# A two-layer decoder kernel: the norms' last step goes from VectorE to GpSimd, two more block loads go ahead of the stores, and two square roots go behind a wide product

## The reference, cut to what matters

```
x = _layernorm(x + self_attention_0(x))          # 16 heads of 8, rotary positions, causal
x = _layernorm(x + cross_attention_0(x, ctx))    # 16 heads of 8, key mask
x = _layernorm(x + experts(x))                   # 8 experts, each token takes 2, hidden width 512
x = _layernorm(x + self_attention_1(x))          # 16 heads of 64, not causal
x = _layernorm(x + cross_attention_1(x, ctx))    # 16 heads of 8, key mask
x = _layernorm(x + ternary_ffn(x))               # weights in {-1, 0, 1}, gelu, an inner norm over 512

def _layernorm(x, axis=-1, eps=1e-05):
    m = jnp.mean(x, axis=axis, keepdims=True)
    v = jnp.var(x, axis=axis, keepdims=True)
    return (x - m) / jnp.sqrt(v + eps)
```

## Time and profile before

| what | us |
|---|---|
| three runs | 410.81, 412.69, 412.75 |
| their median | 412.69 |
| the profiled execution, whole | 409.98 |
| its span, first to last instruction | 408.0 |
| PE busy in the span | 347.2 (85%) |
| DVE busy | 252.6 (62%) |
| POOL busy | 186.3 (46%) |
| ACT busy | 183.7 (45%) |
| mean granted clock of TensorE | 0.946 of full |

### The profile page before, as it was taken

How to read it: one execution, slowest core, us unless ns; L and a number is a source line. 1 busy time by engine, 2 the same in 40 slices (tenths; PEclk the granted TensorE clock), 3 DMA queues, 4 the chain that set the end, 5 groups by cost and what they waited for, 6 DMA issues and landing times.

```text
span 408.0 us, 9801 instructions
## 1 busy us (share of the span) xinstructions
PE 347.2 (85%) x3718; PEld 263.3 (65%) x3718; DVE 252.6 (62%) x592; ACT 183.7 (45%) x386; POOL 186.3 (46%) x267
## 2 busy tenths in 40 slices
PE   3889899998970899898986874899999989999892
PEld 2556666665870889898975561756667565667572
DVE  1799988896554125732353776435566567887894
ACT  2466676664672422222221251433454335667541
POOL 1767666655455245433227633102222247452673
PEclk9999999996996799999996988699999999999998
DMA  6799900000381011111111100000000000000000
GB/s 199 238 307 300 292 2 2 2 2 28 96 261 39 27 53 40 39 40 53 29 31 42 34 19 2 0 2 2 2 2 2 2 2 2 2 2 2 2 26 26
DMA packets 35938, 22.95 MB, mean 56 GB/s; under 512 B 4142, under 2 KB 33846, under 8 KB 35766
## 3 DMA queue, kind: packets, MB, share of 16 engines
q1 hardware_dynamic: 34582, 19.63, 16.7%
q0 software_dynamic: 1024, 2.10, 1.7%
q10 hardware_dynamic: 288, 0.62, 0.5%
HBM read 14.60 MB, written 7.73 MB: 55 GB/s over the span
## 4 chain that ended last, share of the span: by engine, by line
PE 58%; DVE 14%; issue 8%; POOL 7%; ACT 5%; DMA 5%; SPq 1%; POOLq 0%; DVEq 0%; ACTq 0%
PE banks L426 7%; PE banks L821 6%; PE banks L546 5%; PE banks L523 4%; PE banks L1500 4%; PE banks L1508 4%; PE banks L1531 4%; PE banks L808 4%; DMA XG<-routed_rows 3%; PE banks L852 3%; POOL KB L670 2%; PE banks L530 2%; DVE mx L400 2%; PE banks L495 2%; PE banks L507 2%
## 5 line engine op out<-in xcount | busy, mean ns | idle before, releaser
L330 POOL TENSOR_SCALAR ve<-mv 128x1 f32<-128x1 f32 x40 | 10.6, 265 | 93.8 <-DVE mv L325 93.8
L670 POOL TENSOR_TENSOR KB<-KT,cst 128x512 f32<-128x512 f32 x48 | 49.3, 1047 | 7.5 <-DVE KT L630 5.6
L435 ACT ACTIVATE PT<-banks 128x512 f32<-128x512 f32 x64 | 34.9, 595 | 33.3 <-PE banks L426 32.3
L1523 DVE TENSOR_TENSOR PT<-banks,PR 128x512 f32<-128x512 f32 x23 | 15.9, 691 | 46.6 <-PE banks L1508 40.0
L400 DVE TENSOR_REDUCE mx<-banks 128x16 f32<-128x1024 f32 x32 | 38.7, 1209 | 7.9 <-PE banks L530 5.6
L858 ACT ACTIVATE U<-banks 128x512 f32<-128x512 f32 x40 | 23.9, 597 | 42.5 <-PE banks L821 22.1
L426 PE MATMUL banks<-cst,PR 128*128 128x128 f32 x256 | 36.6, 289 | 6.5 <-POOL PR L887 6.5
L1488 POOL COPY U<-WALL 128x1024 f32 x21 | 21.8, 1040 | 43.8 <-PE banks L1508 42.2
L426 PEld LDWEIGHTS banks<-cst,PR 128*128 128x128 f32 x256 | 29.0, 146 | 10.2 <-POOL PR L887 7.6
L808 PE MATMUL banks<-XT,WQKV 128*128 128x128 f32 x256 | 34.9, 300 | 0.4 <-ACT XT L1703 0.4
L416 ACT ACTIVATE PR<-PR 128x1024 f32<-128x1024 f32 x32 | 33.8, 1057 | 3.1 <-DVE PR L410 2.8
(11 more groups left out here) (181 smaller groups left out, 699.1 us busy)
## 6 DMA issues: line engine op xcount, KB each, us to landing
routed_rows<-zero SPq DMA_DIRECT2D x1, 4544.0 KB, 19.1
U<-in_L_ffn_wg_dram SPq DMA_DIRECT2D x8, 256.0 KB, 5.0
U<-in_L_ffn_wu_dram SPq DMA_DIRECT2D x8, 256.0 KB, 5.3
U<-in_L_ffn_wd_dram SPq DMA_DIRECT2D x8, 256.0 KB, 6.0
U<-in_L_attn_W_qkv_dram SPq DMA_DIRECT2D x1, 1536.0 KB, 22.7
XG<-routed_rows SPq DMA_DIRECT2D x23, 64.0 KB, 1.8
routed_rows<-YS SPq DMA_DIRECT2D x23, 64.0 KB, 1.6
cst<-shape_constants ACTq DMA_DIRECT2D x1, 537.0 KB, 4.6
```

Of the source, the lines that this page charges most:

```text
L435: act.activation(PT[:, n % 2, 4 * m:4 * m + 4, :].rearrange("p r q -> p (r q)"), PS[:, B_PT + m, :], ACT.Copy).then_inc(self.pt.sem, 1)
L670: pool.tensor_tensor(KB[:, n % 2, b], bc(KT[:, n % 2, b, :], 1, 8), bc(cst[:, C_HEAD:C_HEAD + 8], 2, SEQ), ALU.mult).then_inc(self.kb.sem, 1)
```

## The change

`apply` moves from VectorE to GpSimd in the narrow, the wide and the ternary stages. It stands right behind the root of the same tile, in the step in which the residual was summed, instead of at the head of VectorE's next step. These are 40 instructions. The eight of the routed stage (L1690) stay on VectorE. `r_dve` gets a wait, since R has two buffers and is now read by another engine: it waits until the tile two back is normed.

SyncE issues six block loads ahead of the first store instead of four. XG keeps its four buffers, so loads 4 and 5 wait for the transposes of blocks 0 and 1.

The roots of the routed stage's tiles 6 and 7 leave the routed stage and stand in step 3 of `post`, behind `shares_pool` of the wide stage's first tile. To make that place, GpSimd's extra work is called twice in a step, and the scatters of the first stream stay where they were.

```
-            def apply(self, dve, i, src):
-                dve.wait_ge(*self.rstd.at(i + 1))
-                dve.tensor_scalar(X[:, i, :], src, mv[:, i % 2, 0:1], rstd[:, i % 2, :],
-                                  ALU.subtract, ALU.mult).then_inc(self.ln.sem, 1)
-                dve.wait_ge(*self.ln.at(i + 1))
+            def apply(self, pool, i, src):
+                pool.wait_ge(*self.rstd.at(i + 1))
+                pool.tensor_scalar(X[:, i, :], src, mv[:, i % 2, 0:1], rstd[:, i % 2, :],
+                                   ALU.subtract, ALU.mult).then_inc(self.ln.sem, 1)
...
+                if job.ago(2):
+                    dve.wait_ge(*job.ago(2).stage.norm.ln.at(job.ago(2).i + 1))
...
-            def ln_dve(self, dve, job):
-                self.norm.apply(dve, job.i, R[:, job.i % 2, :])
-
             def rsqrt_pool(self, pool, job):
                 self.norm.rsqrt(pool, job.i)
+                self.norm.apply(pool, job.i, R[:, job.i % 2, :])
...
-                if x:
-                    x.stage.ln_dve(dve, x)
...
                     t.stage.shares_pool(pool, t)
+                extra(pool, j, False)
                 b = at(tiles, j - 1)
...
-                extra(pool, j)
+                extra(pool, j, True)
...
-                for j in range(4):
+                for j in range(6):
                     load(j)
                 for j in range(BLOCKS):
-                    if j + 4 < BLOCKS:
-                        load(j + 4)
+                    if j + 6 < BLOCKS:
+                        load(j + 6)
...
                     if t + 2 < NT:
                         self.gather(pool, t + 2)
-                    self.rsqrt(pool, t)
-                    self.rsqrt(pool, t + 1)
+                        self.rsqrt(pool, t)
+                        self.rsqrt(pool, t + 1)
...
-        def pre_pool(pool, j):
+        def pre_pool(pool, j, late):
             k = j - DRAIN
-            if k in ROUTED:
+            if late and k in ROUTED:
                 moe.scatter(pool, ROUTED[k])
...
-        def no_pool(pool, j):
-            pass
+        def post_pool(pool, j, late):
+            if j == 3 and not late:
+                for t in (NT - 2, NT - 1):
+                    moe.rsqrt(pool, t)
...
-            stream_pool(pool, post, no_pool)
+            stream_pool(pool, post, post_pool)
```

More of the change, by code:

```diff
@@ L1213, in stream_dve @@
                     y.stage.y_dve(dve, y)
-                t, x = at(tiles, j - 3), turned(tiles, j)
+                t = at(tiles, j - 3)
                 hidden = t and isinstance(t.stage, Ternary)
```

## The result

The changed kernel takes 395.35 us, the median of four runs (394.10 to 401.02). The kernel before took 411.75, the median of four runs beside it. The ratio is 0.961 with a 95% interval of 0.952 to 0.969. Run again later on another chip, it was 401.70 against 415.81: 0.967, 0.963 to 0.972. So it is faster, by 3.3 to 3.9%. I had predicted 399.5 (394.5 to 404).

A forecast was written before the change was run, and what follows sets the result against it. TensorE was taken to bound most stretches, VectorE the rotary norm steps and ternary stage. Terms -7.2 - 4.4 - 1.2 + 1.0 = -11.8 gave 398.2 us from the profiled execution, 400.9 from the median; forecast 399.5, range 394.5 to 404.

The forecast's parts named there:

- Late roots: Wide stage's start: with the roots behind the share, TensorE's wait goes; 7.2 us less (6.5 to 7.8).
- one of my signs of being wrong: Wide stage: third tile's scores starting less than 6 us earlier than before, counted from the stage's start, would mean wrong.
- Loads: Routed stage: six block loads ahead end TensorE's late-load waits except the first; 4.4 us less (3.5 to 5.5).
- all five waits go: 4.4 us: Routed stage: the five load waits after the first, 12.5 - 8.1 = 4.4 us in the table of waits, all vanish.
- Rotary: Two rotary steps with a norm, bound by VectorE: moving `apply` off it saves 1.2 us (0.6 to 1.8).
- The other tiles: Other `apply` tiles up to the ternary stage, beside busy TensorE: no gain, at most 0.6 us in the first stream's drain.
- Ternary: Ternary stage: `apply` on GpSimd lengthens the steps, the tail gives some back; net 1.0 us more (0 to 2.6).
- I take 0.40, bounds 0.22 and 0.6: Assumed time in us of one `apply` on GpSimd, with its lower and upper bounds.
- my own loop: Ternary stage: GpSimd's instructions per steady step, with `apply` at 0.40, summed to 2.7 us against 2.49 before.
- about 0.8 shorter: Ternary stage's tail: without VectorE's `apply` ahead of the next residual, the last chain gets about 0.8 us shorter.
- The rival that gave the drain's clock 3.4 us: First stream's drain: TensorE's clock dip goes, 7.0 us shrink to 3.6, giving 396 us; chance 0.12.
- The base: Whole kernel: starting time between the profiled 409.98 us and the runs' median 412.69; 1.0 us either way.

The follow-up runs named there:

- the version with the last eleven on DVE: The changed kernel with `apply` back on VectorE for the program's last eleven tiles (eight ternary, three second cross-attention); 392.41 us against 410.30, ratio 0.957.

## Why the prediction was right, and where it was wrong

The time was in the range, at its lower end: 395.35 beside 399.5. Term by term, with the profiled executions:

- *Late roots, -7.2 (6.5 to 7.8): -6.9, in the changed kernel and alone.* The wait went, no other took its place, and the share's margin was 5.6 us where I had said 4. Still one of my signs of being wrong came up: the scores of the wide stage's third tile are 5.6 us earlier and not 6, counted from its first scores (27.1 us against 32.7). The projections ahead of the share took 5.84 us there, where they had taken 4.38 before, since TensorE's lower clock lasted longer. In the version with the last eleven on DVE they take 4.36, with the same wait of 1.83 us behind them, and "wide 1-4" is 38.8, 8.4 less than before and more than my upper bound. So the mechanism was right, and that the size was met owes something to luck.
- *Loads, -4.4 (3.5 to 5.5): -6.4, mis-sized.* The mechanism was right, and all five waits went. The failed step is "all five waits go: 4.4 us": I took the idle time of the table as the price. With the same 543 matmuls between the first and last gate TensorE is also busy for 2.0 us less (64.3 before, 62.3 after). Gates behind a late load came 3.57 to 4.41 us after the last, against 2.79: 5.6 us for the five, 1.2 more than the table has. Matmuls start 0.11 us apart here and last 0.28 each, so the end of the last one in front of a gap counts as busy. And seven more intervals of 2.92 to 3.00 show no wait, against three of 2.87 to 2.93 in the changed kernel, another 0.8 us.
- *Rotary, -1.2 (0.6 to 1.8): -1.3 to -1.4*, in the kernel with it alone as well. *The other tiles, 0 with at most 0.6 in the drain: -0.7*: 0.3 in "narrow" (TensorE's shorter wait), 0.3 in "wide 4-8" and 0.1 in "cross 1". I had put the last two at nothing, and what shortens them wasn't looked into.
- *Ternary, +1.0 (0 to +2.6): +2.4, mis-sized, and +1.05 from the clock.* The price of `apply`, "I take 0.40, bounds 0.22 and 0.6", failed: it is 0.82. I had drawn a line between a copy and a one-element instruction, and the form is neither. By my own loop 0.82 gives 0.42 more than the 2.7 us, 3.1. The measured step is 2.77: from L330 to L332 it is 0.30, not 0.67, since L330 now stands ahead of DVE's L1017 and doesn't wait it out, while from L332 to `apply` it is 0.83, not 0.65. These errors nearly cancel, and the steady steps cost the 1.0 us that I had. The three steps with XR cost 1.3 instead of 0.8 (in the apply-only trace, where the clock adds nothing), since the first had no slack: it is 3.71 us against 3.29. The other failed step is the tail, "about 0.8 shorter". The residual does come 0.8 sooner, but I had left out that the last `apply` itself is dearer (0.5), and the time behind it grows by 0.4: +0.1 instead of -0.8.
- *Sum of these: -6.9 - 6.4 - 2.0 + 2.4 = -12.9. The rest to -13.9 is the drain, -2.2, the +1.05 in the ternary stage, and 0.1 or 0.2 elsewhere.* Of the 2.2 us, 1.6 are busy time at the lower clock and 0.6 idle time. The rival that gave the drain's clock 3.4 us had the size of such a thing right, but its cause, an earlier or a shorter wait, isn't borne out by the later traces. That my sum is only 2.1 us off is partly luck, since the terms were wrong both ways: loads 2.0 and the other tiles 0.7 too little gain, ternary 1.4 too little loss. The bounds of the terms also add up to -8.0 and -15.1, not to the -9.0 that I wrote.
- *The base.* I had put the sum between the profiled execution and the median of the runs. The kernel before ran at 407.6 to 413.4 on one chip and 414.4 to 418.4 on another, so no choice of base could have been good to more than 3 us.

## What to carry to other kernels

Price an instruction that changes engines by a row of the same form on the new engine, and where the trace has none, let the upper bound be a multiple; here 0.40 was 0.82, and a stage in which two engines were in balance came to be bound by the other one. Read a recurring wait from start to start of the work behind it, not from the idle time alone: of 6.4 us the table of waits showed 4.4. And before giving a difference to a change, cut both traces at the same instructions and trace the same program twice, since one stretch differed by 8.0 us here between two traces of one program.

## What the runs showed of the hardware

- A tensor_scalar on GpSimd is far dearer than a copy of the same shape: 0.52 to 0.78 against 0.25 us for 128x128, and 3.3 to 3.6 ns for each further element a row. Taking its scalars from memory instead of as constants costs 0.07 for one and 0.16 for two.
- The lower clock near one and the same short wait of TensorE (1.1 to 1.4 us) lasted 3.4, 6.8 or 17 us in different executions, though TensorE was busy nearly throughout, and it began 0.3 to 2.4 us behind the wait or 6.5 us behind it. The whole drain took 38.7 to 48.3 us, a spread larger than what any part of the change is worth.
- In four of fourteen traces VectorE and ScalarE stood still together for 2 to 3 us in the drain, released by something that the profile calls remote. In two of them, one the changed kernel's second, a stretch of the lower clock of 10.2 us follows right behind; whether the stop brings it isn't shown.
- From the end of the last `apply` to the end of the program, over the store of its tile, it was 2.94 us with that `apply` on GpSimd (three traces), 2.56 on VectorE (nine) and 2.41 on ScalarE (one).
- ScalarE does the norm's last step in 0.48 us and GpSimd in 0.82. VectorE takes 0.31 to 0.37 in the ternary stage, 0.34 to 1.06 in the narrow stages, and 1.92 once, beside a GpSimd instruction of 1.90.
